# A fused RWKV-style layer in fp32: four adds per chunk from VectorE to GpSimd, with new engine orders

## The reference

```
xn  = layernorm(x) * ln1_w + ln1_b
sx  = token before - xn               # the first token's predecessor is a row of state
xxx = tanh((xn + sx * maa_x) @ maa_w1)   # 5 groups of 32
x5[g] = xn + sx * (maa_stack[g] + xxx[g] @ maa_w2[g])     g = k, w, v, r, g
w = exp(-exp(time_decay + tanh(x5[w] @ decay_w1) @ decay_w2))
r, k, v = x5[r] @ Wr.T, x5[k] @ Wk.T, x5[v] @ Wv.T ;  g = silu(x5[g] @ Wg.T)
per head, for t in 0..63:  out_t = r_t . (u * k_t v_t + s) ;  s = k_t v_t + w_t * s
x = x + (groupnorm(out) * g) @ Wo.T
xn2, sx2 = layernorm and shift of x ;  x = x + sigmoid(xr @ Fr.T) * (relu(xk @ Fk.T)^2 @ Fv.T)
```

## Time and profile before

| | |
|---|---|
| median of 3 runs (lowest, highest) | 627.14 us (627.03, 631.15) |
| the profiled execution: span from first to last instruction | 625.9 us; the record gives no other time for it |
| busy: VectorE, TensorE, weight loads, ScalarE, GpSimd | 530.9, 482.9, 268.5, 257.2, 84.2 us |
| VectorE's instructions; the adds of L360 among them | 630; 36, 39.9 us |
| moved by DMA | 55.30 MB, 88 GB/s over the span |

### The profile page before, as it was taken

One profiled execution on the slowest core, in us unless ns is written; L12 is line 12 of the kernel. 1 busy time (PEld: TensorE's weight loads), 2 busy tenths in 40 slices (PEclk: granted clock), 3 DMA queues, 4 the chain that ended last, 5 costly groups with the idle time before them and its releaser, 6 DMA issues.

```text
span 625.9 us, 5759 instructions
## 1 busy us (share of the span) xinstructions
PE 482.9 (77%) x1952; PEld 268.5 (43%) x1952; DVE 530.9 (85%) x630; ACT 257.2 (41%) x529; POOL 84.2 (13%) x115
## 2 busy tenths in 40 slices
PE   2958879887978789878887988788887788538435
PEld 1734534543444336433542554344444444325223
DVE  1467899999999999999999999999999998674321
ACT  3333553543542543463445544426431532231231
POOL 1101103101200131002210122023100310020000
PEclk9979879989998999999998998999999998758669
DMA  8260911950294018600761067204820542000100
GB/s 309 73 139 26 206 46 35 201 144 0 68 212 117 2 50 183 169 2 29 165 159 51 12 157 160 68 0 123 180 67 2 126 103 67 0 2 0 59 0 25
DMA packets 19301, 55.30 MB, mean 88 GB/s; under 512 B 1096, under 2 KB 14536, under 8 KB 16712
## 3 DMA queue, kind: packets, MB, share of 16 engines
q1 hardware_dynamic: 19272, 54.94, 35.3%
HBM read 46.55 MB, written 8.39 MB: 88 GB/s over the span
## 4 chain that ended last, share of the span: by engine, by line
DVE 57%; PE 17%; issue 14%; DMA 5%; ACT 5%; POOL 1%; DVEq 0%; SPq 0%; POOLq 0%; ACTq 0%
DVE kv L403 19%; DVE kv L392 8%; DVE kv L411 7%; PE pc L675 7%; DVE x L352 6%; DMA vrep<-v_scratch 3%; PE pa L668 2%; DVE sx L328 2%; DMA v_scratch<-v_sb 2%; DVE trr L466 2%; DVE sq L452 2%; DVE att L432 1%; PE pb L694 1%; DVE xk L457 1%; DVE xres L446 1%
## 5 line engine op out<-in xcount | busy, mean ns | idle before, releaser
L403 DVE TENSOR_TENSOR_SCAN kv<-w_sb,kv 128x512 f32<-128x512 f32 (+2 forms) x144 | 147.3, 1084 | 0.1
L668 PE MATMUL pa<-x,large_sb 128*128 128x512 f32 (+2 forms) x288 | 121.0, 564 | 9.7 <-DVE x L360 9.1
L392 DVE TENSOR_TENSOR kv<-vrep,k_sb 128x504 f32<-128x504 f32 (+2 forms) x144 | 80.2, 619 | 6.4 <-DMA vrep<-v_scratch 6.4
L668 PEld LDWEIGHTS pa<-x,large_sb 128*128 128x128 f32 x288 | 54.6, 195 | 65.1 <-issue 43.0
L411 DVE TENSOR_TENSOR kv<-kv,r_sb 128x2048 f32<-128x2048 f32 (+2 forms) x36 | 73.8, 2049 | 0.3
L780 PE MATMUL patt<-kv,const_sb 128*32 128x512 f32 (+2 forms) x288 | 38.2, 606 | 31.8 <-DVE kv L411 31.7
L282 POOL TENSOR_SCALAR rs<-var 128x4 f32<-128x4 f32 (+2 forms) x18 | 19.4, 1075 | 311.9 <-ACT xhat L506 182.6
L352 DVE SCALAR_TENSOR_TENSOR x<-pb,vec_sb,sx 128x512 f32<-128x512 f32 (+2 forms) x72 | 46.1, 682 | 7.9 <-PE pb L717 6.5
L717 PE MATMUL pb<-th,w_sb 128*128 128x512 f32 (+2 forms) x108 | 46.6, 555 | 0.0
L296 POOL COPY kv<-s_sb 128x32 f32<-128x32 f32 (+2 forms) x36 | 17.7, 492 | 179.6 <-PE patt L780 179.6
L675 PE MATMUL pc<-large_sb,att 128*128 128x256 f32 x128 | 33.6, 420 | 10.5 <-DVE att L438 10.5
(11 more groups left out here) (81 smaller groups left out, 735.9 us busy)
## 6 DMA issues: line engine op xcount, KB each, us to landing
vrep<-v_scratch SPq DMA_DIRECT2D x12, 2048.0 KB, 12.5
vrep<-v_scratch SPq DMA_DIRECT2D x4, 1536.0 KB, 10.1
x_tok<-in_x SPq DMA_DIRECT2D x6, 512.0 KB, 13.9
v_scratch<-v_sb SPq DMA_DIRECT2D x12, 256.0 KB
xres<-in_x SPq DMA_DIRECT2D x6, 512.0 KB, 4.6
out<-ob SPq DMA_DIRECT2D x6, 512.0 KB, 3.2
vrep<-v_scratch SPq DMA_DIRECT2D x2, 1024.0 KB, 9.6
w_sb<-in_w SPq DMA_DIRECT2D x1, 1024.0 KB, 6.3
```

The source lines that it names most:

```text
L392: ins = dve.tensor_tensor(kv[:, q % 2, d, 0:nb, 1:L], vv[:, G4 * j + d, :, 0:L - 1], kk, ALU.mult)
L403: ins = dve.tensor_tensor_scan(flat, w_sb[:, p, q % HF, 0:nb].rearrange("p b t -> p (b t)"), flat, 0.0, ALU.mult, ALU.add)
L668: ins = pe.matmul(dst[:, m, 0:n], w(a)[:, m * P:(m + 1) * P], src[:, a, 0:n], start=(a == 0), stop=(a == HF - 1))
```

## The change

GpSimd adds `xn` to the mixes of v, k, r and gate (`ad0`, `ad1`, `ad3`, `ad4`), each once `mixed` says that VectorE has made it, and each with a semaphore of its own (`x5_added`) on which the projections wait. VectorE's `a_mix` ends with the two operations of L352. `xnp` with its padding column becomes `xn` without; VectorE subtracts tokens 1 to 63 of each sequence, and GpSimd's `prev1` writes the first token's difference into `sx`, a two-input operation in place of a copy. ScalarE's `xn` waits for the four adds, `prev1` and the first mix of the chunk before. All five orders are new. What `normed` did (weight and bias on ScalarE) is written out at its two places.

```diff
@@ -30,20 +30,19 @@
...
-DVE_ORDER = [("rk", 2), ("out", 4), ("sc0", 2), ("cen", 3), ("bonus", 2), ("rs0", 2), ("shift", 1), ("a1", 2),
-             ("gate", 3), ("sc1", 2), ("mix0", 1), ("res", 3), ("mix1", 1), ("a2", 2), ("mix2", 1), ("rs1", 2),
-             ("sc2", 2), ("mix3", 1), ("rs2", 2), ("shift2", 3), ("a3", 2), ("mix4", 1), ("sc3", 2),
-             ("rs3", 2), ("a0", 1), ("att", 2)]
-PE_ORDER = [("M", 3), ("CB", 2), ("T1", 1), ("VR", 3), ("S0", 2), ("W1", 1), ("X0", 1), ("WO", 3), ("X1", 1),
-            ("P0", 1), ("X2", 1), ("P1", 1), ("X3", 1), ("S1", 2), ("D1", 1), ("T2", 3), ("X4", 1), ("P3", 1),
-            ("RR", 3), ("S2", 2), ("KK", 3), ("D2", 1), ("S3", 2), ("Y2", 3), ("P4", 1)]
-ACT_ORDER = [("w", 2), ("tg", 2), ("sq", 3), ("xn", 1), ("rstd", 3), ("th", 1), ("st", 0), ("v", 1),
-             ("st2", 3), ("k", 1), ("nrm2", 3), ("xn2", 3), ("thd", 1), ("nrm", 0), ("rr", 3), ("kk", 3),
-             ("r", 1)]
-POOL_ORDER = [("prev1", 1), ("s01", 2), ("rd1", 0), ("s02", 2), ("rd2", 3), ("s03", 2), ("s00", 1),
-              ("prev2", 2)]
-SP_ORDER = [("lx", 0), ("so", 4), ("lr", 3), ("vst", 1), ("vl0", 1), ("vl1", 1)]
-LAGS = 4
+DVE_ORDER = [("a0", 2), ("out", 4), ("sc0", 2), ("cen", 3), ("shift", 1), ("bonus", 2), ("a1", 2), ("rs0", 2),
+             ("gate", 3), ("mix0", 1), ("sc1", 2), ("mix1", 1), ("res", 3), ("rs1", 2), ("a2", 2), ("mix2", 1),
+             ("sc2", 2), ("mix3", 1), ("a3", 2), ("shift2", 3), ("mix4", 1), ("sc3", 2), ("rs2", 2),
+             ("rs3", 2), ("rk", 1), ("att", 2)]
+PE_ORDER = [("KK", 4), ("S2", 3), ("S3", 3), ("Y2", 4), ("P4", 2), ("M", 3), ("T1", 1), ("CB", 2), ("VR", 3),
+            ("W1", 1), ("X0", 1), ("S0", 2), ("X1", 1), ("WO", 3), ("P0", 1), ("X2", 1), ("P1", 1), ("X3", 1),
+            ("S1", 2), ("D1", 1), ("T2", 3), ("X4", 1), ("P3", 1), ("RR", 3), ("D2", 1)]
+ACT_ORDER = [("rstd", 3), ("th", 1), ("st", 0), ("v", 1), ("st2", 3), ("k", 1), ("nrm2", 3), ("thd", 1),
+             ("xn2", 3), ("r", 1), ("rr", 3), ("kk", 3), ("w", 1), ("nrm", 0), ("tg", 1), ("xn", 0), ("sq", 2)]
+POOL_ORDER = [("prev1", 1), ("s01", 2), ("ad0", 1), ("ad1", 1), ("s02", 2), ("prev2", 3), ("rd2", 3),
+              ("s03", 2), ("ad3", 1), ("rd1", 0), ("ad4", 1), ("s00", 1)]
+SP_ORDER = [("so", 5), ("vst", 2), ("lx", 0), ("vl0", 2), ("vl1", 2), ("lr", 3)]
+LAGS = 5
...
@@ -93,7 +92,7 @@
...
-        xnp = sb("xnp", [P, HF, NB, L + 1])
+        xn = sb("xn", [P, HF, T])
...
@@ -265,11 +261,11 @@
...
-            def put_prev(c, dst, row, done):
-                if c == 0:
-                    pool.wait_ge(in_prev, 16)
-                nb = extent(c)[0]
-                pool.tensor_copy(dst[:, :, 0:nb, 0], prev_sb[:, row, :, FIRST[c]:FIRST[c] + nb]).then_inc(done, 1)
+            def add_xn(c, n):
+                pool.wait_ge(mixed, 5 * c + n + 1)
+                nt = extent(c)[1]
+                pool.tensor_tensor(x5[:, x5_slot(n), :, 0:nt], x5[:, x5_slot(n), :, 0:nt], xn[:, :, 0:nt], ALU.add).then_inc(x5_added[n], 1)
             def token_scale(c, mean, var, rs, sh, begun, powered, done, var_ready, used):
@@ -297,20 +293,25 @@
             def a_prev(c):
-                if c >= 1:
-                    pool.wait_ge(x5_ready, 4 * c)
-                    pool.wait_ge(d1_done, c)
-                put_prev(c, xnp, 1, prev1_put)
+                if c == 0:
+                    pool.wait_ge(in_prev, 16)
+                else:
+                    pool.wait_ge(mixed, 5 * c)
+                pool.wait_ge(xn_ready, c + 1)
+                nb, n = extent(c)[0:2]
+                first = [ap[:, :, 0:n].rearrange("p a (b t) -> p a b t", t=L)[:, :, :, 0] for ap in (sx, xn)]
+                pool.tensor_tensor(first[0], prev_sb[:, 1, :, FIRST[c]:FIRST[c] + nb], first[1], ALU.subtract).then_inc(prev1_put, 1)
             def c_prev(c):
...
-                put_prev(c, xn2p, 0, prev2_put)
+                nb = extent(c)[0]
+                pool.tensor_copy(xn2p[:, :, 0:nb, 0], prev_sb[:, 0, :, FIRST[c]:FIRST[c] + nb]).then_inc(prev2_put, 1)
...
-                "prev1": a_prev, "prev2": c_prev,
+                "prev1": a_prev, "prev2": c_prev, **{f"ad{n}": (lambda c, n=n: add_xn(c, n)) for n in x5_added},
...
@@ -323,23 +324,23 @@
         def _(dve):
             def a_shift(c, p):
...
-                nb, n = extent(c)[0:2]
+                n = extent(c)[1]
+                seqs = [ap[:, :, 0:n].rearrange("p a (b t) -> p a b t", t=L) for ap in (sx, xn)]
+                dve.tensor_tensor(seqs[0][:, :, :, 1:L], seqs[1][:, :, :, 0:L - 1], seqs[1][:, :, :, 1:L], ALU.subtract).then_inc(sx_ready, 1)
+                dve.wait_ge(sx_ready, c + 1)
...
-                dve.tensor_tensor(sx[:, :, 0:n].rearrange("p a (b t) -> p a b t", t=L),
-                                  xnp[:, :, 0:nb, 0:L], xnp[:, :, 0:nb, 1:L + 1], ALU.subtract).then_inc(sx_ready, 1)
-                dve.wait_ge(sx_ready, c + 1)
...
-                    ins = dve.scalar_tensor_tensor(out=by_seq(mix[:, a, 0:n]), in0=by_seq(sx[:, a, 0:n]), scalar=vec("maa_x", a),
-                                                   in1=xnp[:, a, 0:nb, 1:L + 1], op0=ALU.mult, op1=ALU.add)
+                    ins = dve.scalar_tensor_tensor(out=mix[:, a, 0:n], in0=sx[:, a, 0:n], scalar=vec("maa_x", a),
+                                                   in1=xn[:, a, 0:n], op0=ALU.mult, op1=ALU.add)
...
             def a_mix(c, p, n):
...
-                nb, nt = extent(c)[0:2]
+                nt = extent(c)[1]
...
@@ -352,12 +353,6 @@
...
-                if g == MIX_W:
-                    return
-                dve.wait_ge(mixed, 5 * c + n + 1)
-                dst = x5[:, slot, :, 0:nt].rearrange("p a (b t) -> p a b t", t=L)
-                dve.tensor_tensor(dst, dst, xnp[:, :, 0:nb, 1:L + 1], ALU.add).then_inc(x5_ready, 1)
             def a_rk(c, p):
...
@@ -538,9 +526,15 @@
...
-                    act.wait_ge(x5_ready, 4 * c)
+                    for added in x5_added.values():
+                        act.wait_ge(added, c)
+                    act.wait_ge(prev1_put, c)
+                    act.wait_ge(mix_ready, c)
...
-                normed(c, pa, xnp, "ln1_w", "ln1_b", xn_ready)
+                n = extent(c)[1]
+                for a in range(HF):
+                    ins = act.activation(xn[:, a, 0:n], pa[:, a, 0:n], ACT.Identity, bias=vec("ln1_b", a), scale=vec("ln1_w", a))
+                ins.then_inc(xn_ready, 1)
             def a_tanh(c, p):
...
@@ -723,7 +721,7 @@
...
             def p_unit(c, p, n, name, freed, done):
-                pe.wait_ge(x5_ready, summed_mixes(c, n))
+                pe.wait_ge(x5_added[n], c + 1)
...
@@ -737,12 +735,12 @@
...
-                nf, bf = n // DFOLD, extent(c)[0] // DFOLD
+                nf = n // DFOLD
...
-                                  xnp[:, a, f * bf:(f + 1) * bf, 1:L + 1], start=(a == 0), stop=False)
+                                  xn[:, a, f * nf:(f + 1) * nf], start=(a == 0), stop=False)
...
```

More of the change, by code:

```diff
@@ L141, in build @@
         mean1_ready, var1_ready, xhat_ready, sx_ready, mix_ready = [sem(n) for n in ("mean1_ready", "var1_ready", "xhat_ready", "sx_ready", "mix_ready")]
-        mixed, x5_ready, rk_ready, bonus_ready, sg_ready = [sem(n) for n in ("mixed", "x5_ready", "rk_ready", "bonus_ready", "sg_ready")]
+        mixed, rk_ready, bonus_ready, sg_ready = [sem(n) for n in ("mixed", "rk_ready", "bonus_ready", "sg_ready")]
+        x5_added = {n: sem(f"x5_added{n}") for n in (0, 1, 3, 4)}
         kv_ready, state_ready, rs_ready = [sem(n) for n in ("kv_ready", "state_ready", "rs_ready")]
@@ L171, in x5_slot @@
             return n % 3
-        def summed_mixes(c, n):
-            return 4 * c + (n + 1 if n < 2 else n)
         block = ctx.enter_context(nc.Block())
@@ L487, in _ @@
         def _(act):
[L488 to L494, removed]
             def moments(c, src, mean, var, scratch, mean_ready, var_ready, used):
@@ L625, in c_xn @@
                     act.wait_ge(xk_ready, c)
-                normed(c, pc, xn2p, "ln2_w", "ln2_b", xn2_ready)
+                nb, n = extent(c)[0:2]
+                for a in range(HF):
+                    ins = act.activation(xn2p[:, a, 0:nb, 1:L + 1], by_seq(pc[:, a, 0:n]), ACT.Identity,
+                                         bias=vec("ln2_b", a), scale=vec("ln2_w", a))
+                ins.then_inc(xn2_ready, 1)
             def c_rr(c, p):
```

## The result

The changed kernel takes 641.4 us (640.5 to 643.6, 4 runs) where the kernel before took 627.4 beside it: ratio 1.0206, 95% interval 1.0167 to 1.0245. Slower, as forecast, by 14.0 us instead of 20. The profiled execution has a span of 638.8 us, 12.9 more than before.

The account below looks back on a forecast made before the run. VectorE was taken to bound the kernel in the middle. The span of 625.9 us plus 16.5 (adds), 2 (moved steps) and 1.5 (ramp) gave 645.9, with 1.2 around it 647 us (+3.2%); range 605 to 668.

Parts of the forecast that it names:

- What goes: Four adds leave VectorE per full chunk, each worth 1.25 us: 5.0 us, or 34 us if nothing came in exchange.
- The disputed term: GpSimd's add length, taken as 2.2 us, and how long its reads hold VectorE, taken as 2.1 us per add.
- Rival 1: VectorE isn't held because GpSimd's reads slip in between: 597 us; chance 0.14.
- rival 2: VectorE is held only 1.0 us per add, at 0.5 ns per element read: 617 us; chance 0.12.
- Where each add lands: VectorE instructions behind mix0, mix1, mix3 and mix4 are held 2.1, 1.15, 2.1 and 2.1 us: 7.45 per full chunk.
- The sum of the adds and the ramp: Holds less removed adds, +2.45 us over 6.75 full chunks: +16.5; added latency in chunks 0 and 1: +1.5.
- The moved steps: VectorE's rotated order leaves less work to hide some waits: +0.3 us per full chunk, +2 us in all.
- covers: VectorE work that hides a wait, such as 8.5 us over the 7.1 us chain from mix0 to X0.
- What would show it: Trace signs: adds near 2.2 or 3.3 us, GpSimd busy near 190, VectorE groups up 50 to 60, rounds of 68.

Follow-up runs that it names:

- n_memset: The changed kernel with each of GpSimd's four adds replaced by a memset of the same 128x1024: 588.9 us, ratio 0.9388 against the kernel before.
- n_vec: The changed kernel with its new orders, but the four adds made by VectorE again: 626.2 us, ratio 0.9995 against the kernel before.
- b_ad0: The kernel before with rs1 ahead of mix2 in VectorE's order and the add of mix0 alone on GpSimd: 623.2 us, ratio 0.9910.
- b_ctl: The kernel before with rs1 ahead of mix2 in VectorE's order and nothing else, all adds on VectorE: 627.9 us, ratio 0.9994.
- b_ad01: As b_ad0, with the add of mix1 on GpSimd too: 634.8 us, ratio 1.0093 against the kernel before.
- d_ad04: Against the kernel before: adds of mix0 and mix4 on GpSimd, engine orders rearranged to place them beside PSUM-reading instructions: 617.8 us, ratio 0.9836.

## Why the prediction was right, and where it was off

- **What goes, 5.0 us per full chunk:** right. n_memset's rounds are 5.1 under n_vec's.
- **The disputed term.** Right, with the value taken: VectorE is held, for 2.1 us by an add. GpSimd's length was right too (2.17 in b_ad0, 2.37 with the unpadded `xn`, for 2.2), though one of the rows behind it was not: the slope of the short copies. Rival 1 (not held, 597) is what n_memset shows when nothing is read (589); rival 2's bound of 0.5 ns per element read, from a delay of 16 ns, was a factor of two low. The Trainium skill's rule (SBUF — State Buffer, section "Who interferes with whom") agrees in what collides and for how long: reads do (6.67 us for four scans of 4.56), to the end of the instruction that is under way, writes don't (n_memset). It also has issue order decide who blocks, and there the trace differs: add 3, issued in the first product of `a3`, was passed by three more products and a subtraction.
- **Where each add lands.** 2.1, 1.15, 2.1 and 2.1 were expected, 2.1, 1.26, 1.97 and 2.1 measured: 7.4 for 7.45. With them a round comes out: 65.4 in n_vec, less 5.1, plus 7.4, plus the wait of 0.36 ahead of `out`, is 68.1. Add 3 landed elsewhere than I put it, behind the products and in front of L452 instead of between products; the price was the same.
- **The sum of the adds and the ramp,** +16.5 and +1.5: n_vec against the change gives +15.3 by the medians, +13.2 by the ratios. Each late round does grow by 2.8 us, more than the 2.45 worked out, but not all 6.75 full chunks pay that: in the two profiled executions the rounds that begin with the `shift` of chunk 2, 3 and 4 grow by 1.4, 1.8 and 2.4. The prediction charged every full chunk the same. So 3 to 5 us too much stand here.
- **The moved steps,** +2: n_vec against before is a ratio of 0.9995, -1.1 us by the medians. So 2 to 3 us were put on for covers that held. One middle round of before took 67.2 us, with a wait of 1.6 for Y2 ahead of `out` at a granted clock of 0.95; in n_vec all of the last four take 65.3 to 65.5, two of them at 0.97 and without that wait, where b_ctl (nearly the old orders) has 67.2 at 0.97, so the new orders seem to lose less when the clock falls. Both terms erred the same way, and by the medians they make up the 5.6 by which 647 was too high.
- **What would show it:** adds at 2.2 to 2.4 and 3.2, GpSimd busy 180 (190 expected), groups up by some 50 (50 to 60), rounds of 68.1 (68). The long instruction behind mix3 was not one of L392's products but the first mix of `shift2`. A longest VectorE wait on `prev1` of 0.2.

Left open: why GpSimd gets in at the first boundary between scans, but not between the products of `a3`, in any full chunk. A different reading order or the short time between the products' ends could do it; nothing here tells them apart, and the one copy that did get in between two products (at 320.82, before) was issued in the third of the four.

## What to carry to other kernels

Work handed from VectorE to GpSimd is not free of VectorE. In all of these traces, if GpSimd reads SBUF, a VectorE instruction with two SBUF inputs waits for it to its end and shows as a longer instruction, so look for stretched instructions, not for waits. Look at what stands behind each hand-over: with PSUM-reading instructions behind it one add on GpSimd gained 1.1 us a round, with scans behind it the same add lost 0.8. And look at what stands in front of the hand-over on GpSimd's own queue: in b_ad01 a four-element operation, held off by two-input work, made the add 6 us late.

## What the runs showed of the hardware that I had not expected

- GpSimd's rate for 1024 elements: memset 0.95 us, copy 1.04 us, two-input add 2.17 us (`xnp`, padded) or 2.37 us (`xn`, flat). They stood behind different mixes; whether the layout makes the difference isn't shown.
- A four-element GpSimd operation can take 4.73 us, when it is held off through five VectorE instructions in a row (b_ad01), and 5.87 us through six (d_ad04, `rd1` at 290.90), where nothing that VectorE needed stood close behind it and a scan waited 0.38 us at most.
- GpSimd's writes pass beside VectorE's two-input instructions without a delay to either (memset 0.95 us beside scans that stay at 4.56 for four).
